# One attention and mixture-of-experts kernel: start-up orders, packing, maxima and the last fetches rescheduled together

## Chip, cores and metric

The kernel runs on one core of a Trainium2 chip. The metric is the device time of one execution in microseconds (us), as the median of three runs. Engines are TensorE (PE), VectorE (DVE), ScalarE (ACT), GpSimd (POOL) and SyncE (SP). SP, ACT and POOL each issue DMAs.

## What is computed

The input is x, 32 sequences of 256 tokens of 128 numbers (8192 tokens). The layer norm of x goes into an attention block and into a block of 8 experts, and both results are added to x:

```python
xn = _layernorm(x, axis=-1)
x = x + attn(xn, Wqkv, Wproj, bproj) + ffn(xn, gate_w, gate_b, w1, b1, w2, b2)
# attn: 16 heads of 8, rotary embedding, key j allowed for query i where j <= i and i - j <= 64
# ffn: top 2 of 8 gates, softmax over the two, out += w_e * (gelu(x @ w1[e] + b1[e]) @ w2[e] + b2[e])
```

## The kernel before, in words

**Units.** The 8192 tokens are NT = 64 tiles of 128. A pair b (0 to 31) is one sequence, two tiles. Attention runs in 128 units u, four to a pair (half of the queries times half of the heads). The maxima of the scores are taken first (`scores`: PE at L575 and L582, DVE reduce at L881). Unit by unit, ten units later, the scores are computed again transposed with the maxima subtracted as extra rows of the product (`scoresT`: PE at L608, L612 and L619), exponentiated on ACT (L1048) and multiplied by the values (`pv`: PE at L635).

**Queries and keys.** For each pair, PE projects (L548), DVE rotates (L854 to L865), PE transposes (L559), and ACT, DVE and POOL split the result in three bfloat16 parts (L1015, L872, L1020, and `lo` on POOL at L1111). SP writes the parts to DRAM with six DMAs (`write`, L419 and L421) and reads them back in another layout with four (`load`, L432). SP also stores the values (`vstore`, L385) and loads them per pair (`vload`, L396 and L398).

**Maxima.** For each pair, DVE splits the maxima in three parts (`msplit`), PE transposes them (`turn_m`, L591), ACT copies them (L1028) and issues their store to DRAM (`mput`, L1032); after a wait for that store ACT issues two DMAs that load them into the rows of QK (`mget`, L1040). `scoresT` of the pair's first unit waits for these loads.

**Norm and routing.** The tiles are normed in groups of up to six (`stats` L720 and L723, `norm` on DVE L729 to L735 and, from the third group on, 14 small operations on POOL, L1090 to L1101; `apply` on POOL L1105 and ACT L976). From quarter 18 on the top two experts of each token are found (`route`) and POOL scatters the normed tiles into expert slots with 128 indirect DMAs (`scatter`, L1168). `pack` copies each expert's weights into one DRAM tensor (L407, L409), together with both biases (L401, L403). The b2 row of each expert is written 128 times there, for one copy per partition.

**Experts.** 71 slots of 256 tokens are computed one after another: SP loads tokens and weights (`eload` L455, `wload` L464), PE transposes (`etr`, L673), multiplies up (L686) and down (L699), ACT applies gelu (L1069), DVE adds and scales (L941, L947) and POOL scatters the rows by token into DRAM (L1174).

**The end.** 32 `fetch` DMAs on SP (L474) bring the two expert rows of each token, POOL adds the two (L1179), DVE adds them to xr (`combine`, L955) and SP stores (L479).

**Order.** `schedule()` writes one list of steps, and every engine goes through it in order, taking its own part of each step. Its clock is the quarter q, from FIRST = -22 to 139. `middle` and `late` give what a quarter does after `scoresT(q)` and `pv(q-1)`, with an offset d: the step is for pair (q+d)//4. `scores(q+10)` stands between them. The experts are placed as one block at q = 105, so the attention of pairs 26 to 31 comes after them. `norm_late` and `put` are functions inside `schedule()`. A semaphore wait stands in front of each step's first instruction, so whatever follows on the same engine waits too. PSUM has eight banks: 0 and 1 hold `scores`, 2 and 3 hold `scoresT`.

Of the kernel before, what the change touches and what calls it, by code (L numbers as in the profile page):

```python
# [17 lines left out]
NG = len(GR) - 1  # L18
NB = len(BT) - 1
# [8 lines left out]
FIRST = -22  # L28
ROUTE = 18
# [3 lines left out]
def schedule():  # L33
# [12 lines left out]
    middle = ((("add", 20), ("out", -4), ("mput", 4), ("residual", -8)), (("hi", 19), ("mget", 3)),  # L46
              (("norm_y", -6), ("rest", 18), ("expand", 2)), (("rope", 21), ("mid", 17)))
# [17 lines left out]
    def norm_late(q):  # L65
# [6 lines left out]

        for g in range(3, NG):
            d = FIRST + 4 * (g - 1) - q
            if 6 <= d <= 8:
                order.append(("stats", g, 8 - d))
            if d == 6:
                order.append(("norm", g))
        for g in range(2, NG):
            d = FIRST + 4 * (g - 1) - q  # L80
            order.extend(("apply", g, j) for j, at in enumerate((4, 3, 2, 2, 1, 0)) if d == at)
# [14 lines left out]
    def put(stages, q):  # L96
        order.extend((what, (q + d) // 4) for what, d in stages[q % 4] if 0 <= (q + d) // 4 < NP)
# [7 lines left out]
    for q in range(FIRST, NU + 12):  # L105
        if q == 4 * CUT + 1:
            order.append(("up", 0))
            for i in range(NS):
                if 4 <= i + 3 < NS:
                    order.extend([("eload", i + 3), ("wload", i + 3)])  # L110
                if i + 2 < NS:
                    order.append(("etr", i + 2))
                if i + 1 < NS:
                    order.append(("up", i + 1))
                order.append(("down", i))
# [12 lines left out]
        put(late, q)  # L128
        norm_late(q)
# [16 lines left out]
        for n in pieces(k - 3):  # L146
# [8 lines left out]
def attention_moe_kernel(nc, x, wqkv, wproj, bproj, gate_w, gate_b, w1, b1, w2, b2, cf, cb, out):  # L155
# [15 lines left out]

    Dst = [nc.dram_tensor(f"stack_{i}", (2, 6, P, 256), bf16).ap() for i in range(3)]
# [5 lines left out]
    Wd = nc.dram_tensor("experts", (NE, P, WE), f32).ap()  # L178

# [3 lines left out]
    with ctx:  # L183
# [112 lines left out]
        d_vl = [semaphore(f"d_vl{i}") for i in range(NV)]  # L296
        d_b, d_bt, e_bt, a_bt, v_wv = (semaphore(n) for n in ("d_b", "d_bt", "e_bias", "a_bias", "v_wv"))
# [43 lines left out]
        yv = Ys[ROW0:, :].rearrange("(t p a) c -> p t a c", p=P, a=2)  # L341
# [8 lines left out]

        def bank(n):
            return (7, 4)[n] if n < 2 else 6 - n % 2

# [17 lines left out]
        def _(e):  # L371
            for g in range(NG):
                e.dma_start(xr[:, GR[g]:GR[g + 1], :], xv[:, GR[g]:GR[g + 1], :]).then_inc(d_x[g], 16)  # L373
            for what, *a in ORDER:
                if what == "ones":
                    e.wait_ge(p_cb, 1)
                    for n in range(NQ):
                        for g in range(2):
                            e.dma_start(QK[64 * g + 48:64 * g + 51, n, 1, :].rearrange("p (r c) -> p r c", c=P),
                                        onesb[0:3, :].unsqueeze(1).broadcast_to((3, 16, P))).then_inc(d_one, 16)  # L380
                elif what == "vstore":
                    n = a[0]
                    u0, m = BT[n], BT[n + 1] - BT[n]
                    e.wait_ge(a_vp, n + 1)
# [14 lines left out]
                elif what == "bias" and a[0] == 2:  # L399
# [3 lines left out]
                    e.dma_start(Wd[:, :, 1028:WE], b2s[:, 0:1, :].broadcast_to((NE, P, P))).then_inc(d_bt, 16)  # L403
                elif what == "pack":
                    ex = a[0]
                    if a[1] == 0:
# [59 lines left out]
                elif what == "fetch":  # L466
# [7 lines left out]
                    e.dma_start(gy[:, k % NF, :, :, :], yv[:, 2 * b:2 * b + 2, :, :]).then_inc(d_g[k % NF], 16)  # L474
# [8 lines left out]
        def _(e):  # L483

            b4, b5, b6, b7 = [], [], [], []
            for what, *a in ORDER:
# [106 lines left out]
                elif what == "scoresT":  # L593
                    b, t, c = a[0] // 4, a[0] // 2 % 2, a[0] % 2
                    s = b % NQ
                    e.wait_ge(d_m[b % 2], 32 * (b // 2 + 1))
                    if a[0]:
# [642 lines left out]
```

## Time and profile before

| what | us |
| --- | --- |
| median of 3 runs | 747.93 (747.35 to 749.89) |
| profiled execution, whole | 751.46 |
| its span, first to last instruction | 749.3 |
| PE, DVE, ACT, POOL busy in the span | 655.8, 479.8, 358.3, 391.8 |
| mean granted PE clock | 0.951 of full |

The span is taken from the trace, and the execution's own time is 2.2 us longer. A busy share is an average over stages that have different limits: the start (to 58 us, where the first `scores` runs), attention beside norm and routing (58 to 209 us), attention beside the scatters (209 to 403 us), the experts (to 673 us) and the last attention units beside the fetches (to 749.3 us).

### The profile page before, as it was taken

To read this page: it belongs to the slowest core of one execution; us is meant where nothing else is said; L and a number is where in the kernel's file an instruction comes from. 1 tells how busy PE (TensorE), PEld (TensorE's weight loads), DVE (VectorE), ACT (ScalarE), POOL (GpSimd) and SP (SyncE) were. 2 spreads that over 40 slices of the span, in tenths; PEclk is the share of its full clock that TensorE was granted. 3 is DMA by queue.
4 is the path that set the end of the run, shared out by engine and by line. 5 is a ranking of instruction groups with operands and counts; after the bars stand their busy time and mean duration, and the time that the engine had idled before them with its cause. 6 is when DMAs were issued, how large, how long until landed. Compare 5 with 4: busy or idle time off the path is not lost.

```text
span 749.3 us, 26576 instructions
## 1 busy us (share of the span) xinstructions
PE 655.8 (88%) x10238; PEld 527.9 (70%) x10238; DVE 479.8 (64%) x1362; ACT 358.3 (48%) x681; POOL 391.8 (52%) x525
## 2 busy tenths in 40 slices
PE   7436799978799898899989799999999999998866
PEld 3324576655566676566657799999999999995654
DVE  6538987699778878777887344444444444446654
ACT  1322576645355555455556344444444444455443
POOL 1563544056777776777660355555555554553344
PEclk8788999999799999999999999999999999999886
DMA  9567899764777877877778777777767676866797
GB/s 259 143 119 209 218 240 258 195 165 133 203 194 211 221 211 191 220 183 203 190 191 246 212 232 232 234 233 236 231 227 234 230 232 208 254 197 159 200 281 240
DMA packets 161436, 158.78 MB, mean 212 GB/s; under 512 B 20328, under 2 KB 140280, under 8 KB 161312
## 3 DMA queue, kind: packets, MB, share of 16 engines
q1 hardware_dynamic: 147504, 136.12, 64.7%
q0 software_dynamic: 8640, 17.97, 7.2%
q10 hardware_dynamic: 5168, 3.00, 1.5%
q8 instruction: 82, 1.34, 0.8%
q14 instruction: 42, 0.34, 0.1%
HBM read 102.06 MB, written 59.06 MB: 215 GB/s over the span
## 4 chain that ended last, share of the span: by engine, by line
PE 54%; DMA 13%; DVE 11%; SPq 8%; issue 7%; ACT 4%; POOL 3%; ACTq 1%; DVEq 0%; POOLq 0%
PE ps L699 17%; PE ps L686 16%; DMA maxima<-mT 9%; DVE mx L881 4%; PE ps L635 4%; POOL slots_x L1168 2%; PE ps L663 2%; SPq L419 2%; SPq L373 2%; PE ps L575 2%; ACT PT L1048 2%; PE ps L619 2%; PE ps L673 2%; PE ps L548 2%; DMA stack<-sp 2%
## 5 line engine op out<-in xcount | busy, mean ns | idle before, releaser
L1174 POOL DMA_INDIRECT chosen_y<-xn,to x142 | 135.9, 957 | 141.3 <-DVE xn L947 117.2
L881 DVE TENSOR_REDUCE mx<-ps 128x8 f32<-128x1024 f32 x128 | 156.4, 1222 | 67.1 <-PE ps L582 65.7
L1048 ACT ACTIVATE PT<-ps 128x1024 f32<-128x1024 f32 x128 | 131.0, 1023 | 135.3 <-PE ps L619 69.2
L1069 ACT ACTIVATE hb<-ps,xn 128x256 f32<-128x256 f32 x284 | 116.6, 470 | 150.9 <-PE ps L686 150.8
L1168 POOL DMA_INDIRECT slots_x<-xn,pos x128 | 125.4, 980 | 55.9 <-issue 33.3
L699 PEld LDWEIGHTS ps<-xn,hb 128*128 128x128 f32 x1136 | 138.7, 193 | 3.7
L699 PE MATMUL ps<-xn,hb 128*128 128x128 f32 x1136 | 138.8, 276 | 0.0
L686 PE MATMUL ps<-xn 128*128 128x256 f32 x568 | 135.4, 381 | 0.0
L686 PEld LDWEIGHTS ps<-xn 128*128 128x128 f32 x568 | 102.9, 191 | 11.2
L941 DVE TENSOR_TENSOR xn<-ps,xn 128x256 f32<-128x256 f32 x71 | 30.1, 424 | 100.3 <-PE ps L699 100.3
L635 PE MATMUL ps<-PT,V 128*32 128x64 f32 (+1 forms) x3072 | 87.8, 247 | 2.7 <-issue 2.7
L575 PE MATMUL ps<-cb_s 64*64 64x512 bf16 x512 | 54.4, 410 | 22.4 <-DMA QK<-stack 12.8
L635 PEld LDWEIGHTS ps<-PT,V 128*32 128x32 f32 x3072 | 58.4, 113 | 12.4 <-issue 2.9
L1111 POOL TENSOR_TENSOR sp<-rr,sp 128x512 bf16<-128x512 f32 x32 | 37.2, 1163 | 48.8 <-ACT sp L1020 48.4
L582 PEld LDWEIGHTS ps<-QK 48*64 48x64 bf16 x2048 | 47.1, 109 | 15.9 <-issue 4.5
L582 PE MATMUL ps<-QK 48*64 48x128 bf16 x2048 | 54.3, 221 | 2.2 <-issue 2.1
L619 PE MATMUL ps<-QK 51*128 51x64 bf16 (+1 forms) x1536 | 53.0, 202 | 1.1 <-issue 1.1
L619 PEld LDWEIGHTS ps<-QK 51*128 51x128 bf16 x1536 | 45.9, 97 | 11.4 <-issue 2.9
L575 PEld LDWEIGHTS ps<-cb_s 64*64 64x64 bf16 x512 | 15.3, 104 | 44.5 <-issue 39.7
L548 PE MATMUL ps<-wq_s,xnT 128*128 128x256 f32 x128 | 40.6, 445 | 6.8 <-ACT Vt L989 6.4
L1179 POOL TENSOR_TENSOR xn<-xn 128x256 f32<-128x256 f32 x32 | 23.9, 760 | 34.1 <-DMA xn<-chosen_y 34.1
L933 DVE TENSOR_TENSOR to<-eq,cf_s 128x2 int32<-128x2 f32 x71 | 11.5, 161 | 40.9 <-DMA chosen_y<-xn,to 39.4
(133 smaller groups left out, 902.2 us busy)
## 6 DMA issues: line engine op xcount, KB each, us to landing
xn<-experts SPq DMA_DIRECT2D x71, 578.0 KB, 3.9
QK<-stack SPq DMA_DIRECT2D x128, 192.0 KB
stack<-sp SPq DMA_DIRECT2D x64, 192.0 KB
xn<-slots_x SPq DMA_DIRECT2D x71, 132.0 KB, 3.4
stack<-sp SPq DMA_DIRECT2D x64, 128.0 KB
xn<-chosen_y SPq DMA_DIRECT2D x32, 256.0 KB, 4.6
stack<-sp SPq DMA_DIRECT2D x64, 64.0 KB
Vc<-values SPq DMA_DIRECT2D x32, 128.0 KB
```

The costliest lines, as they stand in the source:

```text
L548: k = e.matmul(ps[:, 5, t * 256:(t + 1) * 256], xnT[:, c0:c0 + P], wq_s[:, 0:256], start=True, stop=True, skip_group_check=True)
L575: e.matmul(ps[q0:q0 + 64, g, :].rearrange("p (h k) -> p h k", h=4), unit[r:r + 64, 0:64], (win0 if t + blk == 0 else win)[r:r + 64, :].uns ...
L582: k = e.matmul(ps[q0 % P:q0 % P + m, g, h4 * P:(h4 + 1) * P], qk_rows(0, g, 48, s, hh, q0, m), qk_rows(1, g, 48, s, hh, w0, P), start=Fals ...
L619: k = e.matmul(ps[:, 2 + g, h4 * P + q0 % P:h4 * P + q0 % P + m], qk_rows(1, g, 51, s, hh, w0, P), qk_rows(0, g, 51, s, hh, q0, m), start= ...
L635: k = e.matmul(ps[32 * j:32 * j + 32, 4, o0:o0 + n], V[:, b % NV, w, 4 * g + j, 16 * c:16 * c + 32], PT[:, a[0] % 2, i0:i0 + n], start=t + ...
L686: k = e.matmul(ps[:, 2 * s + c // 2, (c % 2) * SL:(c % 2 + 1) * SL], w1b[:, i % NW, c * P:(c + 1) * P], xsT[:, i % 3, :], start=True, stop ...
L699: k = e.matmul(ps[:, bk, j * P:(j + 1) * P], hb[:, s, c, j * P:(j + 1) * P], w2b[:, i % NW, c * P:(c + 1) * P], start=c == 0, stop=c == 3, ...
L881: e.tensor_reduce(mo[:, :, :, c, t], ps[:, 0:2, :].rearrange("p g (h k) -> p g h k", k=P), AX.X, ALU.max, negate=True).then_inc(v_mx, 1)
L1048: e.activation(PT[:, u % 2, :], ps[:, 2:4, :].rearrange("p c k -> p (c k)"), ACT.Exp, scale=SCALE).then_inc(a_exp, 1)
L1069: e.activation(hb[:, s, c, :], ps[:, 2 * s + c // 2, (c % 2) * SL:(c % 2 + 1) * SL], ACT.Gelu, bias=b1b[:, i % NW, c:c + 1]).then_inc(a_ge ...
L1168: e.indirect_dma_start(out=Xs, out_offset=bass.IndirectOffsetOnAxis(ap=pos[:, n, u:u + 1], axis=0), in_=xn[:, u, :], in_offset=None).then_ ...
L1174: e.indirect_dma_start(out=Ys, out_offset=bass.IndirectOffsetOnAxis(ap=to[:, i % 4, j:j + 1], axis=0), in_=yb[:, i % 4, j, :], in_offset=N ...
```

## The change

It consists of these edits, all in one kernel:

- **Norm.** `stats` of groups 4 to 8 are issued two thirds of a group per quarter, from q = -19 to -12; before they were one third per quarter and lasted to q = 0. The `norm` steps work on groups 0, 1, 2, 3, then 4 and 5 together, 6 to 8 together, 9 and 10 (NR). `factors(g)` gives the waits. The `apply` steps of group 2 on ACT are put later.
- **SP's queue at the start.** The eight `ones` DMAs go from SP at q = -19 to ACT, one per quarter from q = -9. The first two `vstore` DMAs are issued by ACT right behind their copies.
- **Packing.** `pack` goes from one DMA per quarter (q = 1 to 16) to one every third quarter. The 512 KB write of b2 from SBUF is replaced by a 4 KB store to DRAM at the start and a broadcast from DRAM to DRAM at q = 49.
- **Maxima.** `mget` goes from q = 4b-3 to q = 4b-2. For pairs 28 to 31 `turn_m`, `mput` and `mget` stand at q = 4b-6, 4b-5 and 4b-3, in place of 4b-5, 4b-4 and 4b-3.
- **Entry to the experts.** `load` and `vload` of q = 103 are held back until slot 2 of the experts, behind `eload` and `wload` of slot 5.
- **Last ten units.** `scoresT` of units 118 to 127 alternates between banks 2, 3 and banks 0, 1 (`stb`), so it waits for the exponential of the unit before the last.
- **Fetches.** The rows of DRAM are laid out so that one partition reads 2 KB in one piece. Two fetches per quarter begin at the seventh fetch instead of the eleventh, and the `combine` steps follow four quarters behind instead of three.

```diff
+NR = (0, 1, 2, 3, 4, 6, 9, 10, 11)
+FREE = 28
-    middle = ((("add", 20), ("out", -4), ("mput", 4), ("residual", -8)), (("hi", 19), ("mget", 3)),
-              (("norm_y", -6), ("rest", 18), ("expand", 2)), (("rope", 21), ("mid", 17)))
+    middle = ((("add", 20), ("out", -4), ("mput", 4), ("residual", -8)), (("hi", 19),),
+              (("norm_y", -6), ("rest", 18), ("mget", 2), ("expand", 2)), (("rope", 21), ("mid", 17)))
...
-        for g in range(3, NG):
-            d = FIRST + 4 * (g - 1) - q
-            if 6 <= d <= 8:
-                order.append(("stats", g, 8 - d))
-            if d == 6:
-                order.append(("norm", g))
+        d = q - FIRST
+        some = [(3, d)] if d < 3 else [divmod(n, 3) for n in (2 * d + 6, 2 * d + 7) if n < 27]
+        some += [(g, 8 - FIRST - 4 * (g - 1) + q) for g in (9, 10) if 6 <= FIRST + 4 * (g - 1) - q <= 8]
+        for g, p in some:
+            order.append(("stats", g, p))
+            if p == 2 and g + 1 in NR:
+                order.append(("norm", NR.index(g + 1) - 1))
...
-        if q == FIRST + 3:
-            order.append(("ones",))
+        if -9 <= q < -9 + 2 * NQ:
+            order.append(("ones", q + 9))
-        if 1 <= q <= 2 * NE:
-            order.append(("pack", (q - 1) // 2, (q - 1) % 2))
+        if q >= 1 and q % 3 == 1 and q // 3 <= 2 * NE:
+            order.append(("pack", q // 3 // 2, q // 3 % 2))
...
+    def maxima(q):
+        for what, d in (("mput", 5), ("turn_m", 6), ("mget", 3)):
+            if (q + d) % 4 == 0 and FREE <= (q + d) // 4 < NP:
+                order.append((what, (q + d) // 4))
     def pieces(k):
-        return [k] if 0 <= k < 10 else [n for n in (2 * k - 10, 2 * k - 9) if n < NP] if k >= 10 else []
+        return [k] if 0 <= k < 6 else [n for n in (2 * k - 6, 2 * k - 5) if n < NP] if k >= 6 else []
...
+                if i == 2:
+                    order.extend(held)
...
+        maxima(q)
+        if q == 4 * CUT - 1:
+            held = [o for o in order if o in (("load", (q + 13) // 4), ("vload", (q + 5) // 4))]
+            order = [o for o in order if o not in held]
...
-        for n in pieces(k - 3):
+        for n in pieces(k - 4):
...
+    TWO = NU - AHEAD
+        def stb(u):
+            return 0 if u >= TWO and (u - TWO) % 2 else 2
...
-                    e.dma_start(Wd[:, :, 1028:WE], b2s[:, 0:1, :].broadcast_to((NE, P, P))).then_inc(d_bt, 16)
+                    e.dma_start(b2d, b2s[:, 0, :]).then_inc(d_b2, 16)
                 elif what == "pack":
                     ex = a[0]
-                    if a[1] == 0:
+                    if ex == NE:
+                        e.wait_ge(d_b2, 16)
+                        e.dma_start(Wd[:, :, 1028:WE], b2d.unsqueeze(1).broadcast_to((NE, P, P))).then_inc(d_bt, 16)
...
-                    e.dma_start(gy[:, k % NF, :, :, :], yv[:, 2 * b:2 * b + 2, :, :]).then_inc(d_g[k % NF], 16)
+                    e.dma_start(xflat[:, k % NF * 512:(k % NF + 1) * 512], yv[b]).then_inc(d_g[k % NF], 16)
...
-                    if a[0]:
+                    if a[0] == TWO + 1:
+                        e.wait_ge(v_mx, NU)
+                    elif a[0] > TWO + 1:
+                        e.wait_ge(a_exp, a[0] - 1)
+                    elif a[0]:
                         e.wait_ge(a_exp, a[0])
...
+                elif what == "ones":
+                    n, g = divmod(a[0], 2)
+                    e.wait_ge(p_cb, 1)
+                    e.dma_start(QK[64 * g + 48:64 * g + 51, n, 1, :].rearrange("p (r c) -> p r c", c=P),
+                                onesb[0:3, :].unsqueeze(1).broadcast_to((3, 16, P))).then_inc(d_one, 16)
...
-                         2.0 * (np.arange(64)[None, :] * 128 + np.arange(128)[:, None]) + ROW0,
+                         2.0 * (np.arange(64)[None, :] // 2 * 256 + np.arange(64)[None, :] % 2 + 2 * np.arange(128)[:, None]) + ROW0,
```

## Rows read from the trace of the kernel before

**Rows 1.** Busy us (x instructions) of each engine by stage, granted clock, DMA share, GB/s

```profile
58.00:86.00 28.00, 19.76 (x300) 14.53 (x300) 26.17 (x76) 10.93 (x25) 13.59 (x37) 0.94 0.79 209
86.00:152.00 66.00, 59.98 (x1302) 44.80 (x1306) 51.07 (x123) 42.71 (x77) 23.49 (x59) 0.97 0.88 230
152.00:209.00 57.00, 45.72 (x1016) 31.71 (x1017) 47.16 (x99) 26.34 (x41) 35.14 (x45) 0.91 0.60 159
209.00:390.00 181.00, 164.19 (x4055) 117.08 (x4049) 146.74 (x256) 102.58 (x159) 130.43 (x131) 0.99 0.76 205
...
419.00:673.00 254.00, 254.00 (x1758) 239.66 (x1757) 116.63 (x536) 111.45 (x272) 127.28 (x133) 0.99 0.72 229
673.00:714.00 41.00, 34.89 (x841) 25.34 (x843) 26.60 (x49) 19.80 (x29) 14.66 (x18) 0.92 0.65 175
714.00:749.30 35.30, 23.74 (x447) 16.70 (x447) 16.56 (x41) 14.23 (x20) 15.13 (x20) 0.73 0.89 265
```

**Rows 2.** Chain that ended last, 20 to 58 us: start us, us, what

```profile
19.42 6.38 DMA values<-Vt
...
37.34 4.75 SPq L419
...
50.01 2.31 DMA stack<-sp
...
53.65 4.30 DMA QK<-stack
```

**Rows 3.** DMA view of 36 to 49 us, in 40 slices

```profile
DMA  0599754444444444444469644444447495445434
GB/s 0 147 235 228 30 21 54 46 50 46 47 46 50 46 47 46 50 46 47 46 120 221 106 46 50 46 47 46 50 46 98 55 195 68 49 54 66 46 41 39
```

**Rows 4.** Timeline of SP, 0 to 130 us: start us, us, engine line operation

```profile
26.80 6.22 SPq L379 DMA_DIRECT2D QK<-cb_s  x8
...
54.58 1.79 SPq L419 DMA_DIRECT2D stack<-sp  x3
56.41 1.55 SPq L421 DMA_DIRECT2D stack<-sp  x3
```

**Rows 5.** Timeline of all engines, 0 to 62 us: POOL's rows

```profile
19.43 0.20 POOL L1090 TENSOR_TENSOR nw<-rs 128x6 f32<-128x6 f32 x1 [6.58 <-DVE rs L735]
...
23.47 0.20 POOL L1101 TENSOR_SCALAR nb<-nb 128x6 f32<-128x6 f32 x1
...
34.20 1.16 POOL L1111 TENSOR_TENSOR sp<-rr,sp 128x512 bf16<-128x512 f32 x1 [3.07 <-ACT sp L1020]
```

**Rows 6.** Groups by line, 58 to 86 us: busy, mean ns | idle before

```profile
L720 DVE BATCH_NORM_STATS2 bst<-xr 128x6 f32<-128x128 f32 x16 | 3.8, 278 | 0.0
```

**Rows 7.** Waits, 209 to 390 us: us in total, times, longest

```profile
ACT PT L1048 <- DMA maxima<-mT: 34.1, 12, 3.5
```

**Rows 8.** What PE at L608 sat idle for, 209 to 390 us

```profile
  ACT PT L1048: 6.5, 10
```

**Rows 9.** Timeline, 208 to 222 us: a load of maxima, and its user

```profile
215.24 0.57 ACTq L1040 DMA_DIRECT2D QK<-maxima  x2
...
219.48 0.11 PEld L612 LDWEIGHTS ps<-cb_s 64*128 64x128 bf16 x4
```

**Rows 10.** Groups by line, 209 to 390 us: the scatters

```profile
L1168 POOL DMA_INDIRECT slots_x<-xn,pos x115 | 112.3, 977 | 51.4 <-issue 30.2 <-PE ps L582 20.0 <-ACT sp L1020 1.2
```

**Rows 11.** Timeline of PE, 409 to 427 us: the stall behind the first slots

```profile
418.63 0.41 PE L673 MATMUL ps<-cf_s,xn 128*128 128x128 f32 x2 [3.81 <-DMA xn<-slots_x]
```

**Rows 12.** Waits, 674 to 749 us

```profile
POOL xn L1179 <- DMA xn<-chosen_y: 34.1, 18, 6.4
...
ACT PT L1048 <- DMA maxima<-mT: 11.1, 3, 4.0
```

**Rows 13.** Timeline, 715 to 750 us: PE behind the last such wait

```profile
728.22 0.61 PE L608 MATMUL ps<-cb_s 64*128 64x512 bf16 x2 [2.88 <-ACT PT L1048]
```

**Rows 14.** Waits of the whole span: DVE on landed expert rows

```profile
DVE to L933 <- DMA chosen_y<-xn,to: 39.4, 43, 3.3
```

More of the change, by code:

```diff
@@ L96, in put @@
     def put(stages, q):
-        order.extend((what, (q + d) // 4) for what, d in stages[q % 4] if 0 <= (q + d) // 4 < NP)
+        for what, d in stages[q % 4]:
+            if 0 <= (q + d) // 4 < (FREE if what in ("turn_m", "mput", "mget") else NP):
+                order.append((what, (q + d) // 4))
+    def maxima(q):
+        for what, d in (("mput", 5), ("turn_m", 6), ("mget", 3)):
+            if (q + d) % 4 == 0 and FREE <= (q + d) // 4 < NP:
+                order.append((what, (q + d) // 4))
     def pieces(k):
-        return [k] if 0 <= k < 10 else [n for n in (2 * k - 10, 2 * k - 9) if n < NP] if k >= 10 else []
+        return [k] if 0 <= k < 6 else [n for n in (2 * k - 6, 2 * k - 5) if n < NP] if k >= 6 else []
     moved, due = 0, 0.0
@@ L178, in attention_moe_kernel @@
     Wd = nc.dram_tensor("experts", (NE, P, WE), f32).ap()
+    b2d = nc.dram_tensor("bias_2", (NE, P), f32).ap()
     Ys = nc.dram_tensor("chosen_y", (ROW0 + 2 * NT * 128, P), f32).ap()
@@ L296, in attention_moe_kernel @@
         d_vl = [semaphore(f"d_vl{i}") for i in range(NV)]
+        d_b2 = semaphore("d_b2")
         d_b, d_bt, e_bt, a_bt, v_wv = (semaphore(n) for n in ("d_b", "d_bt", "e_bias", "a_bias", "v_wv"))
@@ L349, in xn_ready, with factors @@
             return (p_xn, 3 * g + ON_POOL.index(j) + 1) if j in ON_POOL else (a_xn, 3 * g + ON_ACT.index(j) + 1)
+        def factors(g):
+            return max(i for i in range(len(NR)) if NR[i] <= g) - 1
         def bank(n):
             return (7, 4)[n] if n < 2 else 6 - n % 2
+        def stb(u):
+            return 0 if u >= TWO and (u - TWO) % 2 else 2
         def batch(u):
@@ L374, in _ @@
             for what, *a in ORDER:
[L375 to L381, printed above, removed]
+                if what == "vstore":
                     n = a[0]
                     u0, m = BT[n], BT[n + 1] - BT[n]
+                    if n < 2:
+                        continue
                     e.wait_ge(a_vp, n + 1)
@@ L725, in _ @@
                     g = a[0]
[L726 removed]
+                    u0, u1 = GR[NR[g]], GR[NR[g + 1]]
                     y, a_, b_ = nw[:, 0, u0:u1], nw[:, 1, u0:u1], rs[:, u0:u1]
@@ L991, in _ @@
                                  ACT.Copy).then_inc(a_vp, 1)
+                    if n < 2:
+                        e.wait_ge(a_vp, n + 1)
+                        e.dma_start(Vd.rearrange("(t p) c -> p t c", p=P)[:, BT[n]:BT[n + 1], :],
+                                    Vt[:, n % 2, 0:m * P].rearrange("p (t c) -> p t c", c=P)).then_inc(d_vs[n % 2], 16)
                 elif what == "expand":
@@ L1047, in _ @@
                         e.wait_ge(e_pv, u - 1)
-                    e.activation(PT[:, u % 2, :], ps[:, 2:4, :].rearrange("p c k -> p (c k)"), ACT.Exp,
+                    e.activation(PT[:, u % 2, :], ps[:, stb(u):stb(u) + 2, :].rearrange("p c k -> p (c k)"), ACT.Exp,
                                  scale=SCALE).then_inc(a_exp, 1)
```

17 lines of the change are left out of this document (9 added, 8 removed).

## The prediction

> **What bounds the kernel now.** I first cut the span into stages with the view of busy time by window [rows 1]. The experts (419 to 673 us) are PE alone: 254.00 of 254 us busy, at clock 0.99. No edit takes work from that stage, so a third of the time can't move unless DMA gets in its way. Everything to be won lies before and after it. Then I read the chain that ended last in each stage, to see what it hangs on, and the waits and the timeline for the price of each link.
>
> At the start the chain leaves the engines: it is the store of the first values (6.38 us to landing), then SP's issue of the first `write`, whose first DMA alone holds SP for 4.75 us, then its landing and the first `load`, landed at 57.95 us [rows 2]. From 58 to 86 us DVE is the bound, 26.2 of 28 us busy; from 86 to 152 us it is PE (60.0 of 66) with DMA at 0.88; from 152 to 209 us DVE carries the routing (47.2 of 57). From 209 to 390 us PE is busy 164.2 of 181 us, and POOL nearly as much: 130.4 us, plus 30.2 us of issue gaps that stand before its scatters whatever PE does [rows 1, 10]. In the last 76 us PE is busy 58.6 us and the clock falls to 0.73 in the second part [rows 1].
>
> **The change part by part.**
>
> *First write.* Today SP spends 6.22 us on the `ones` DMAs [rows 4] and then sends b2. After that, for some eight microseconds, the DMA view stands at 4 to 5 tenths and 46 to 50 GB/s [rows 3]: half of the 16 DMA engines work, slowly. 512 KB at 47 GB/s are 11.2 us, and the six DMAs of `write` take SP from 37.34 to the last one's issue at 50.01, where an unhindered write needs 1.79 + 1.55 = 3.4 us [rows 2, 4]. That b2 is the cause I infer from its size. The edit takes away all three: `ones`, b2, and (with the stores of the values on ACT) the place of the values behind the x loads. I take the values' landing 3.4 us earlier, half of the 6.38 us that it took [rows 2], between nothing and all of it. But POOL gets a new step in front: `norm` of groups 4 and 5 now stands before the first `lo`, and such a norm takes 4.2 us (19.43 to 23.67) on POOL [rows 5]. So `lo`, now at 34.20, would be at 34.2 - 3.4 + 4.2 = 35.0 if DVE had the statistics ready; DVE must do six more pairs of tiles before it, and I put `lo`'s end at 38.7 us. Then 3.4 us of issue, 2.3 - 0.5 to landing, 1.7 of issue of the loads and 4.3 - 0.4 to landing give about 49.8 us against 57.95. **-8 us** (bounds -3, if only b2's obstruction is half gone, and -13, if `lo` keeps to 35.0).
>
> *Statistics out of DVE's tight stage.* From 58 to 86 us 16 tiles' statistics fall, 3.8 us at L720, with aggregation at some two thirds of that again, about 6.3 us in all (an estimate), and the small norm operations [rows 6]. They move to before 58 us, where SP and DMA hold the chain [rows 2]. DVE being the bound, this would give 6; PE and the turn-taking of PE and DVE over banks 0 and 1 take the rest. **-4** (-1 to -7).
>
> *Packing thinned, 86 to 152 us.* DMA falls from 0.88; PE, 60.0 of 66 us busy, leaves 6 at most [rows 1]. **-3** (0 to -6). In the routing stage nothing moves but `mget`: **-1** (0 to -4).
>
> *Maxima, 209 to 390 us.* ACT waits 34.1 us in 12 places because `mget` stands in its queue while the store of the maxima is still on its way, and the exponential is behind it [rows 7]. That looks like the prize, but PE works on meanwhile: it pays 6.5 us in 10 places [rows 8]. With `mget` one quarter later the exponential goes first. POOL would then be next: 115 scatters and the `lo`s fill 181 - 20.0 = 161 us, so the stage can't shrink by more than 20, and 16.8 us is PE's own idle time [rows 1, 10]. **-6** (0 to -15).
>
> *b2 again, q = 49.* The broadcast has the same 8 x 128 x 512 bytes, now in the midst of attention. The `load` behind it, two quarters later, has three quarters (8 us) until it is used and needs about 4.3 [rows 2]; a queue of 11.2 us would be half over. **+1** (0 to +8).
>
> *Here a rule speaks against the change.* The row shows half of the DMA share while b2 is out [rows 3]. The Trainium skill, "DMA: Bandwidth & Descriptors", section "Why a DMA increments its semaphore by 16 and not by 1", says that a DMA from SP or ACT is spread over the largest number of DMA engines, up to 16, that divides the slowest dimension on both sides; by that rule, the trace agrees, and the broadcast from DRAM, whose slowest dimension is still 8, keeps 8 engines. The sum would have +8 there by the rule at its hardest, and +1 by my reading.
>
> *Entry to the experts.* PE stands 3.81 us before slot 4's tokens, because SP is held by `load` and `vload`, behind `write` [rows 11]. Holding these loads frees SP. **-4** (-2 if the slot's own tokens still come late, -6 if the clock, which falls where PE pauses as in the last stage [rows 1], comes back sooner too).
>
> *The end.* For pairs 28 to 31 the store of the maxima leaves one quarter earlier, so ACT's waits (11.1 us, 3 times [rows 12]) go; here PE is not full and pays nearly all, 2.88 us at the last [rows 13]: 8.5 us. Two banks for the last ten units and the higher clock of a busier PE give some 4 more, since now each exponential and each `scoresT` take turns. Against that stands DMA, 0.89 busy at 265 GB/s in the last 35 us [rows 1]: this fixes how fast fetches and stores go by, and POOL already waits 34.1 us for fetches [rows 12]. Pieces of 2 KB help. **-9** (-3 to -14).
>
> *At nothing:* `apply` of group 2 moved (ACT waits there anyway), `ones` on ACT (eight issues in quarters in which ACT is busy 10.9 of 28 us [rows 1]); without that cover, 6 us.
>
> **Sum:** -8 - 4 - 3 - 1 - 6 + 1 - 4 - 9 = -34. The profiled execution's own time is 751.5, giving 717.5; it stands 3.5 us above the median of the runs, so the median becomes 747.9 - 34 = **714**.
>
> **The rivals.**
>
> 1. *Maxima come late.* They are now asked for closer to their use. Today 3.7 us lie between the end of the issue (215.81) and the first use (219.48) with no wait shown [rows 9], so landing takes less, but PE would be 0.7 us sooner. If landing takes 3.5 us, PE waits about as long as it gained, and the 7 us of stages 152 to 390 are not won: 721; with stores that take longer, 724.
> 2. *b2 obstructs in its new place* as in the old one, +8 instead of +1: 721.
> 3. *The end is bound by DMA.* The attention units run ahead and then wait for fetches; -3 instead of -9: 720. For: the share of 0.89. Against: only 0.65 before 714 us, and fetches that start denser there [rows 1].
> 4. *More is won:* PE's idle time of 209 to 390 us goes nearly whole and the end gives 14: 714 - 9 - 5 = 700.
> 5. *Slower.* The new layout puts the rows that L1174 scatters further apart. DVE already waits 39.4 us for their landing [rows 14], and DVE has to be done with a slot in 3.7 us (1758 PE instructions at 26 per slot are 68 slots in 254 us), of which it is busy 1.7 [rows 1]. If landing grew by over 2 us, PE would start to wait, 71 times; at another 0.6 us per slot that is +43, and 757. Nothing shows it: the rows stay 512 bytes.
>
> **Chances.** Forecast 0.55 (own range 705 to 724); rivals 1 and 2 0.12 and 0.10; rival 3 0.10; rival 4 0.08; rival 5 0.03; several of 1 to 3 at once and more give-backs, ending near 730 or at no change, 0.02. The range runs from 700 to 731. A measurement of this kernel tells about 0.3% (2.2 us) from no change. Faster 0.95, same 0.02, slower 0.03.
>
> **What would show it.** First `scores` at about 50 us; its `write` in 3.4 us of SP. DVE under 0.85 busy in the ten quarters after. ACT's wait for the store of maxima nearly gone from 209 us on, PE over 0.94 busy and the scatters without a wait for PE. No stall of 3.8 us behind the first slots. From the last slot to the end about 67 us instead of 76, clock above 0.85. Wrong would be: a wait of L612 for QK<-maxima in most pairs (rival 1), a `scores` that waits for QK<-stack near q = 53 (rival 2), an unchanged 76 us at the end with POOL waiting for fetches (rival 3), slots of over 3.8 us (rival 5).

## The result and the profile after

The changed kernel takes **728.49 us** (median of four runs, 721.15 to 731.24), the kernel before 747.64 (four runs, 746.68 to 749.89): a ratio of 0.9719, interval 0.9666 to 0.9772. Forecast were 714 in a range of 700 to 731. The sign and the range held, the size did not: about 19 to 20 us were won where 34 were said. The four runs of the changed kernel lie 10 us apart, those of the kernel before 3.

The clearest ruler for a kernel in which one engine does 128 like steps is the time at which given steps start. The exponentials on ACT (one per attention unit) are such steps. The profile of before, timeline of ACT, the exponentials of units 0, 20, 36, 100 and 127 (the experts come between 104 and 108); a line ends with ACT's idle time before it and what ended it:

```profile
85.74 1.02 ACT L1048 ACTIVATE PT<-ps 128x1024 f32<-128x1024 f32 x1
...
152.01 1.02 ACT L1048 ACTIVATE PT<-ps 128x1024 f32<-128x1024 f32 x1 [1.79 <-PE ps L619]
...
209.39 1.02 ACT L1048 ACTIVATE PT<-ps 128x1024 f32<-128x1024 f32 x1 [1.72 <-PE ps L619]
...
392.00 1.03 ACT L1048 ACTIVATE PT<-ps 128x1024 f32<-128x1024 f32 x1 [0.85 <-PE ps L619]
...
739.31 1.02 ACT L1048 ACTIVATE PT<-ps 128x1024 f32<-128x1024 f32 x1 [0.51 <-PE ps L619]
```

And of after (the line is L1095 there; the same units):

```profile
75.47 1.02 ACT L1095 ACTIVATE PT<-ps 128x1024 f32<-128x1024 f32 x1
...
137.00 1.02 ACT L1095 ACTIVATE PT<-ps 128x1024 f32<-128x1024 f32 x1 [1.79 <-PE ps L656]
...
194.27 1.02 ACT L1095 ACTIVATE PT<-ps 128x1024 f32<-128x1024 f32 x1 [1.54 <-PE ps L656]
...
379.40 1.03 ACT L1095 ACTIVATE PT<-ps 128x1024 f32<-128x1024 f32 x1 [0.90 <-PE ps L656]
...
716.97 1.02 ACT L1095 ACTIVATE PT<-ps 128x1024 f32<-128x1024 f32 x1 [0.18 <-PE ps L656]
```

Their differences, with the first `scores` (58.08 us before, 50.05 after) and the ends of the spans (749.3 and 729.0), give a table that adds up to the whole:

| stretch | before | after | difference | forecast |
|---|---|---|---|---|
| start to the first `scores` | 58.1 | 50.1 | -8.0 | -8 |
| to exponential 0 | 27.7 | 25.4 | -2.2 | -4 |
| exponentials 0 to 20 | 66.3 | 61.5 | -4.7 | -3 |
| 20 to 36 | 57.4 | 57.3 | -0.1 | -1 |
| 36 to 100 | 182.6 | 185.1 | +2.5 | -6 + 1 |
| 100 to 104 | 10.3 | 10.2 | -0.2 | |
| 104 to 108, the experts between | 282.0 | 279.1 | -2.8 | -4 |
| 108 to 127 | 55.0 | 48.3 | -6.7 | -9, with the next |
| 127 to the end | 10.0 | 12.0 | +2.0 | |
| sum | 749.3 | 729.0 | -20.3 | -34 |

(Differences are taken before rounding. The profiled execution of after took 731.24 us, the slowest of its four; that of before, 751.46, was the slowest too.) So 7.5 of the 13.7 missing us are lost between exponentials 36 and 100, and 4.3 after 108.

The engines by stage in after answer to [rows 1]; columns as there:

```profile
50.00:75.30 25.30, 20.35 (x279) 14.98 (x279) 20.70 (x37) 10.62 (x24) 9.33 (x11) 0.88 0.78 208
75.00:137.00 62.00, 59.14 (x1334) 44.44 (x1332) 50.65 (x118) 43.19 (x78) 21.27 (x46) 1.00 0.86 215
137.00:194.00 57.00, 45.43 (x1018) 31.72 (x1021) 47.24 (x99) 26.53 (x41) 35.37 (x45) 0.91 0.68 186
194.00:379.00 185.00, 166.10 (x4084) 119.25 (x4078) 147.65 (x257) 106.13 (x160) 130.24 (x132) 0.97 0.80 212
391.00:660.00 269.00, 265.38 (x1849) 250.32 (x1847) 123.74 (x566) 119.32 (x288) 132.38 (x139) 1.00 0.73 229
660.00:729.00 69.00, 49.88 (x1261) 35.11 (x1259) 44.25 (x86) 32.54 (x47) 28.32 (x37) 0.92 0.80 238
```

In the second row PE is busy 59.1 of 62 us: that stage is now PE's. In the fourth it still stands 18.9 us, in the last 19.1.

The chain of after, 20 to 60 us, beside [rows 2]: from POOL's last norm operation and `lo` to the first `scores`, with no gap for b2.

```profile
38.21 1.13 POOL sp L1158
39.36 0.38 SPq L451
...
41.52 0.69 SPq L453
42.25 1.72 DMA stack<-sp
...
44.82 1.44 SPq L464
46.30 3.62 DMA QK<-stack
50.05 0.64 PE ps L607 x4
```

`write` now needs 2.9 us from first issue to landing's start (12.7 us before). **Waits** of 194 to 379 us, beside [rows 7] and [rows 8]:

```profile
POOL slots_x L1215 <- issue: 30.1, 91, 4.9
PEld ps L607 <- issue: 24.0, 37, 3.9
ACT V L1042 <- DMA Vc<-values: 19.6, 11, 3.6
...
PE ps L607 <- issue: 12.7, 8, 3.7
...
ACT V L1042 <- DMA maxima<-mT: 3.6, 3, 1.6
PE ps L607 <- DMA QK<-stack: 2.9, 2, 1.5
```

ACT's wait for the store of the maxima, 34.1 us in 12 places before the exponential, is down to 3.6 in 3, all before another instruction. In its place ACT waits 19.6 us for `values`, and PE stands in front of L607, the first matmul of `scores`, 15.6 us in 10 places (12.7 + 2.9), most of its idle time; before the change it stood 2.8 us in front of that matmul (L575) from exponential 36 to 100. SP's own waits between exponentials 36 and 100 say what the `load` came behind. In the kernel before, L428 is its wait for a free QK buffer and L432 that for the landed `write`:

```profile
SPq L428 <- PE ps L619: 27.7, 14, 4.7
...
SPq L432 <- DMA stack<-sp: 8.8, 9, 1.7
```

and in after (L460 and L464):

```profile
SPq L464 <- DMA stack<-sp: 25.6, 14, 2.9
SPq L460 <- PE ps L656: 23.1, 13, 4.3
```

### The profile page after: what moved, and what is told of

Read it like the earlier page. It is cut to its first block, busy times and chain, and to the rows that moved or that the text cites. A ratio compares the mean times of both kernels' runs of the same rounds, so it can differ in the third digit from the quotient of the medians.

```text
span 729.0 us, 26522 instructions
## 1 busy us (share of the span) xinstructions
PE 648.6 (89%) x10234; PEld 523.8 (72%) x10238; DVE 479.2 (66%) x1353; ACT 360.9 (50%) x681; POOL 385.0 (53%) x483
## 4 chain that ended last, share of the span: by engine, by line
PE 67%; DVE 15%; DMA 6%; issue 6%; SPq 3%; POOL 2%; ACTq 0%; ACT 0%; DVEq 0%; POOLq 0%
PE ps L736 17%; PE ps L723 16%; PE ps L672 7%; DVE mx L918 6%; PE ps L607 5%; PE ps L614 3%; PE ps L580 3%; PE ps L656 3%; PE ps L700 2%; PE ps L649 2%; PE ps L710 2%; PE ps L591 2%; DMA QK<-stack 2%; PE ps L645 1%; DMA stack<-sp 1%
## 5 line engine op out<-in xcount | busy, mean ns | idle before, releaser
L1095 ACT ACTIVATE PT<-ps 128x1024 f32<-128x1024 f32 x128 | 131.0, 1023 | 89.6 <-PE ps L656 82.9
L672 PE MATMUL ps<-PT,V 128*32 128x64 f32 (+1 forms) x3072 | 85.3, 244 | 4.6 <-ACT PT L1095 1.8
L607 PE MATMUL ps<-cb_s 64*64 64x512 bf16 x512 | 54.3, 413 | 26.9 <-issue 15.1
L672 PEld LDWEIGHTS ps<-PT,V 128*32 128x32 f32 x3072 | 57.1, 111 | 15.4 <-ACT PT L1095 3.4
L1158 POOL TENSOR_TENSOR sp<-rr,sp 128x512 bf16<-128x512 f32 x32 | 37.7, 1178 | 55.8 <-ACT sp L1062 55.3
L656 PEld LDWEIGHTS ps<-QK 51*128 51x128 bf16 x1536 | 45.0, 96 | 10.2 <-issue 1.3
L607 PEld LDWEIGHTS ps<-cb_s 64*64 64x64 bf16 x512 | 15.5, 104 | 47.2 <-issue 43.0
L970 DVE TENSOR_TENSOR to<-eq,cf_s 128x2 int32<-128x2 f32 x71 | 11.5, 161 | 43.3 <-DMA chosen_y<-xn,to 41.4
L1226 POOL TENSOR_TENSOR xn<-xn 128x256 f32<-128x256 f32 x32 | 23.6, 756 | 29.8 <-DMA xn<-chosen_y 29.6
```

Of the source, the lines that this page charges most:

```text
L607: e.matmul(ps[q0:q0 + 64, g, :].rearrange("p (h k) -> p h k", h=4), unit[r:r + 64, 0:64], (win0 if t + blk == 0 else win)[r:r + 64, :].uns ...
L656: k = e.matmul(ps[:, B + g, h4 * P + q0 % P:h4 * P + q0 % P + m], qk_rows(1, g, 51, s, hh, w0, P), qk_rows(0, g, 51, s, hh, q0, m), start= ...
L672: k = e.matmul(ps[32 * j:32 * j + 32, 4, o0:o0 + n], V[:, b % NV, w, 4 * g + j, 16 * c:16 * c + 32], PT[:, a[0] % 2, i0:i0 + n], start=t + ...
L1095: e.activation(PT[:, u % 2, :], ps[:, stb(u):stb(u) + 2, :].rearrange("p c k -> p (c k)"), ACT.Exp, scale=SCALE).then_inc(a_exp, 1)
```

## The experiments

These ran on chips on which the kernel before took longer than the 747.6 us above: 796.5 us for the first four runs (13 runs of before), 793.6 for the next four, 758.1 for the last four. Ratios are to those; stage times are best compared within such a group. The first group and the last ran on a chip that bears the same number, so "a slower chip" stands below for a slower group of runs: whether it was another chip or another hour isn't shown. Only the first group has a run of the changed kernel as it is, and none has a profile of the kernel before. The profile of the changed kernel in the first group differs in one stage above all: exponentials 36 to 100 take 222.9 us instead of 185.1.

**The changed kernel again.**

> The changed kernel unaltered, as the reference for the runs beside it. Its four runs so far spread from 721.2 to 731.2 us, so I expect a median of 721 to 731. Quarter 36 to quarter 100 took 185.1 us in its profile (before: 182.6); if that is the kernel's own rhythm and no accident of one execution, it is again 180 us or more. First scores at 50 us, and a loss of 3 us or more between quarters 44 and 56, behind the broadcast of b2.

776.90 us, ratio 0.9729 (0.9649 to 0.9808): the same gain, on a chip 6.5% slower, so the 721 to 731 us expected missed. Exponentials 44 to 56 took 42.9 us. First `scores` 48.8 us, exponential 0 at 73.9, span 775.0. In its waits, 185 to 408 us, PE and ACT stand in other places than above:

```profile
POOL slots_x L1215 <- PE ps L614: 64.9, 46, 2.7
ACT PT L1095 <- remote: 25.9, 11, 2.7
...
PEld ps L607 <- issue: 20.4, 60, 1.1
```

The longest wait before L607 is 1.1 us, against 3.9: here many small stalls bind, not a few long ones. What a run of this group says of stage 36 to 100 doesn't carry over to the faster chip without a doubt.

**Maxima: back to three quarters' lead, and moved alone.**

```diff
-              (("hi", 19),), (("norm_y", -6), ("rest", 18), ("mget", 2), ...
+              (("hi", 19), ("mget", 3)), (("norm_y", -6), ("rest", 18), ...
```

> The changed kernel with the loads of the maxima (pairs below 28) asked for three quarters ahead again. Theory A (from quarter 36 on the bound is now the round trip of queries and keys through DRAM: lo, write, load, scores; the exponential was free anyway): ACT's wait for the store of the maxima is back at 30 us or more, and the time stays within 3 us of the changed kernel. Theory B (my prediction's: the exponential held up behind mget costs PE 0.6 us a pair): 6 us or more slower. Theory C (maxima asked for late make scoresT wait): 3 us or more faster.

778.65 us, 0.9723 (0.9663 to 0.9783): no difference from the changed kernel. ACT's wait for the store was only 7.5 us in this run (30 or more were expected), since units come more slowly on this chip (3.5 us each in that stage, 2.9 on the faster), so this doesn't price the edit where the wait is 34 us.

The other way round, `("mget", 2)` in place of `("mget", 3)` as the one edit to the kernel before:

> The kernel before with one edit: the loads of the maxima asked for two quarters ahead. Theory A: ACT's wait of 51.7 us for the store of the maxima nearly goes, and the whole becomes at most 3 us faster (745 or more). Theory B: 6 to 12 us faster (736 to 742). Theory C: slower, with a wait of L612 for the loads of the maxima.

794.77 us, 0.997 (0.9928 to 1.0012; ten runs). Moved alone it brings nothing that can be measured on this chip; there the 2.7% are won by the rest. PE waits 3.9 us in two places at L612 for `QK<-maxima`, the sign of rival 1; in the profile of after it doesn't.

This run is also the nearest thing to a profile of the kernel before in this group (its profiled execution, 787.8 us, is 7 us faster than its median). Beside the changed kernel (`after_again`) its stages read:

| stretch | `mget_alone` | `after_again` |
|---|---|---|
| start to exponential 0 | 85.0 | 73.9 |
| exponentials 0 to 20 | 61.8 | 61.6 |
| 36 to 100 | 223.4 | 222.9 |
| 104 to 108, the experts between | 280.4 | 286.4 |
| 108 to the end | 62.5 | 59.1 |

So what the start wins here (11.0 us) is as much as the two profiles differ in all (10.6). Between exponentials 0 and 20 the packing and the statistics stand where they stood before, and still the stretch is only 0.2 us longer. And the experts take 6.0 us more in the changed kernel: with the loads in their old place, PE never waited for a slot's tokens here; with them held, it waits 2.7 us.

**b2: sent in the start after all.** The broadcast to the eight experts stands again where it did, the changed kernel otherwise as it is.

```diff
+ e.dma_start(Wd[:, :, 1028:WE], b2s[:, 0:1, :].broadcast_to((NE, P, P))).then_inc(d_bt, 16)
  e.dma_start(b2d, b2s[:, 0, :]).then_inc(d_b2, 16)
...
- e.dma_start(Wd[:, :, 1028:WE], b2d.unsqueeze(1).broadcast_to((NE, P, P))).then_inc(d_bt, 16)
+ pass
```

> The changed kernel with the 512 KB write of b2 from SBUF back at the start, and nothing at quarter 49. If that write alone held up the first write of the stack: first scores at 57 to 60 us instead of 50. If the broadcast at quarter 49 costs what the profile shows (some 4.6 us between quarters 44 and 56), these come back, and the whole is 3 to 5 us slower than the changed kernel; if the loss there has another cause, 8 to 10 us slower. If the removal of the ones DMAs from SP was what mattered at the start, no change there and 4 us faster in all.

783.06 us, 0.980 (0.9737 to 0.9864). The timeline of SP:

```profile
33.59 4.92 SPq L433 DMA_DIRECT2D bias<-b2s  x1
38.56 7.74 SPq L452 DMA_DIRECT2D stack<-sp  x3
46.34 1.78 SPq L454 DMA_DIRECT2D stack<-sp  x3
```

`write` takes SP 9.6 us, behind 4.9 for the small store of b2 that stands between (in the kernel before, with nothing between, `write` took 13.1), and the first `scores` come at 55.3 instead of 48.8 us: **6.5 us** for this one DMA. Exponential 0 comes 6.6 us later and the span ends 4.8 us later. That b2 was the cause, inferred from its size only, is shown.

**b2 over 16 engines.** In its new place (q = 49) the broadcast with partitions as the outer dimension instead of experts.

```diff
- e.dma_start(Wd[:, :, 1028:WE], b2d.unsqueeze(1).broadcast_to((NE, P, P))).then_inc(d_bt, 16)
+ e.dma_start(Wd[:, :, 1028:WE].rearrange("e p c -> p e c"),
+             b2d.unsqueeze(0).broadcast_to((P, NE, P))).then_inc(d_bt, 16)
```

> The changed kernel with the broadcast of b2 at quarter 49 written with the 128 copies as the slowest dimension instead of the 8 experts. If the loss between quarters 44 and 56 comes from that DMA filling the queues of 8 of the 16 DMA engines: the DMA view shows no stretch at half share there, and the time from quarter 44 to quarter 56 drops by 2 us or more; whole 0.965 to 0.970 of the kernel before (changed kernel: 0.972). If the loss is only jitter of the round trip of queries and keys: no change beyond 1 us in the mean.

778.41 us, 0.9774 (0.9697 to 0.9852): the whole doesn't tell them apart. Between exponentials 44 and 56, where the broadcast falls, it took 40.6 us, against 41.8 to 44.0 in the three other kernels of its group, which all have the broadcast over 8 experts. In the first group it was 42.9 and 42.8 with that broadcast, and 41.6 and 42.1 in the two kernels that send b2 in the start. So about 1 us hangs on the broadcast in the first group, and 1 to 3 on its form in the second, each from single profiles.

**Packing every quarter again.** `pack` in quarters 1 to 16 instead of every third.

```diff
-        if q >= 1 and q % 3 == 1 and q // 3 <= 2 * NE:
-            order.append(("pack", q // 3 // 2, q // 3 % 2))
+        if 1 <= q <= 2 * NE:
+            order.append(("pack", (q - 1) // 2, (q - 1) % 2))
+        if q == 49:
+            order.append(("pack", NE, 0))
```

> The changed kernel with the 16 packing DMAs in quarters 1 to 16 again, one each, and b2 at quarter 49 as it is. My prediction's step: quarter 0 to quarter 20 takes 3 us more than the changed kernel's 61.5 us. Rival: the DMAs only moved their load into the stage that lives on the round trip through DRAM, so that quarters 20 to 48 become 2 to 4 us shorter and the whole stays at 0.972.

780.54 us, 0.9789 (0.9706 to 0.9871). Exponentials 0 to 20 took 62.8 us instead of the 61.6 of two others in this group: thinning is worth about 1.2 us here, less than the 3 forecast. `mget_alone`, with the old packing, took 61.8, so it may be less still. Exponentials 20 to 48 took 103.1 us against 101.9 to 103.6 in the others: the rival's 2 to 4 us less aren't there.

**`lo` and `write` one quarter earlier.** The round from `lo` through DRAM to the `load` gets a quarter more.

```diff
-    late = ((("turn_qk", 20), ("lo", 16)), (("turn_o", -5), ("msplit", 7), ("write", 15)),
-            (("qk", 22), ...), (("load", 13), ..., ("turn_m", 5)))
+    late = ((("turn_qk", 20), ("write", 16)), (("turn_o", -5), ("msplit", 7)),
+            (("qk", 22), ...), (("load", 13), ..., ("turn_m", 5), ("lo", 17)))
```

> The changed kernel with lo right behind mid, ahead of that quarter's scatters, and its write one quarter earlier. Theory A (the round trip lo, write, load, scores bounds quarters 36 to 100, and it begins late because lo stands behind scatters on POOL): SP's wait of 37.9 us for the landed write in front of the loads falls by half or more, quarters 36 to 100 take 175 us or less instead of 185, whole 0.960 of before or less. Rival D (the loads wait for the QK buffer, that is for scoresT three quarters before their use, whatever the write does): same 185 us.

785.59 us, 0.9868 (0.979 to 0.9945): slower than the two runs above (its fastest, 784.9 us, against their slowest, 783.5). The first `scores` come at 45.03 us, 3.0 earlier than in `b2_on_16`, and exponential 0 at 68.57, 4.9 earlier, but 36 to 100 (189.65 to 424.76) takes 235.1 us instead of the 220.4 to 223.3 of the others in its group. SP's wait for the landed `write`, only 9.4 us in all in `after_again`, is 5.7 here, and its wait for a free QK buffer goes from 84.6 to 151.8. So on this chip it is rival D's wait that stands in front of the loads, and theory A's forecast of a faster stage missed.

The start still has 3 to 5 us to give; why the middle pays 12 or more for it isn't settled (POOL, which runs both `lo` and the scatters, gets them in another order).

**`scores` nine quarters ahead instead of ten.** `load` gets a quarter more to land before its use.

```diff
-AHEAD = 10
+AHEAD = 9
...
-  (("turn_o", -5), ("msplit", 7), ("write", 15)), (("qk", 22), ("turn_y", -6))
+  (("turn_o", -5), ("write", 15)), (("qk", 22), ("msplit", 6), ("turn_y", -6))
```

> The changed kernel with scores nine quarters ahead of scoresT instead of ten (msplit one quarter later). This gives each load one more quarter until its first scores, and takes one from the maxima. Theory A and rival D both: PE's waits in front of L607 (36.7 us from quarter 36 to 100) nearly go, and the stage takes 175 us or less. If POOL's scatters are the bound (they wait for scores, which come one quarter later), the stage stays at 185 us. If the maxima become the bound, ACT waits for their store again by 30 us or more.

785.10 us, 0.9869 (0.9772 to 0.9967). 36 to 100 took 222.3 us, as in the others, and the wait for issue before L607 in that stretch stayed: 26.2 us (21.2 of weight loads, 5.0 of matmuls) against 29.2 in `after_again`. One quarter more in front of the `load` brings nothing on such a chip, whose stalls there are the short ones.

**No held load.** `load` and `vload` go out in their place, in front of the expert slots' tokens.

```diff
         if q == 4 * CUT - 1:
-            held = [o for o in order if o in (("load", ...), ("vload", ...))]
-            order = [o for o in order if o not in held]
+            held = []
```

> The changed kernel without holding back load and vload at the entry to the experts. My prediction's step: the stretch from the first transpose of a slot to the last down product (268.9 us in the changed kernel's profile, 271.6 before) becomes 4 us longer, with a wait of slot 4 for its tokens. Rival: the held loads only move the stall to slot 6 (2.8 us there), so without them the stretch changes by 1 to 3 us, either way, and where SP happens to be early it gets shorter, to the 266 us without any stall.

738.51 us, 0.9763 (0.9704 to 0.9822; before 758.05). PE's timeline behind the first slots, beside [rows 11]:

```profile
410.37 0.66 PE L712 MATMUL ps<-cf_s,xn 128*128 128x128 f32 x2 [5.24 <-DMA xn<-slots_x]
```

The stall is back, 5.24 us, and from the first expert transpose to the last `down` 273.4 us pass, against 269.4 and 271.3 in the next two runs and 268.9 in the profile of after: the holding is worth 2 to 4 us in this group. In the first group a kernel without it (`mget_alone`) had no such stall at all, and its block took 4.4 us less than that of `after_again`, so the gain isn't shown for that chip.

**One bank for the last ten units.**

```diff
-    return 0 if u >= TWO and (u - TWO) % 2 else 2
+    return 2
```

(with the matching waits: every unit waits for the exponential before it).

> The changed kernel with all scoresT in banks 2 and 3. My prediction's step: units 116 to 127 take 3 to 4 us more than the 25.2 to 25.5 us of the changed kernel, and the whole 3 us more. Rival (the end hangs on the fetches): the units take longer, but from the last exponential to the end it is then less than the 12.0 us of the changed kernel, so that the whole changes by under 2 us.

731.12 us, 0.9689 (0.961 to 0.9767). Units 116 to 127 take 26.5 us, 1 us more where 3 to 4 were forecast (27.8 in `no_hold`, which has the two banks), and from exponential 108 to the end 57.8 us pass (`no_hold`: 59.9, after: 60.3). The two banks bring nothing that can be seen. This was one of the two things that the forecast's term for the end rested on.

**Fetches sooner.** The pairs of fetches begin after two single ones instead of six, and `combine` waits one quarter longer.

```diff
-        return [k] if 0 <= k < 6 else [n for n in (2 * k - 6, 2 * k - 5) if n < NP] if k >= 6 else []
+        return [k] if 0 <= k < 2 else [n for n in (2 * k - 2, 2 * k - 1) if n < NP] if k >= 2 else []
...
-        for n in pieces(k - 4):
+        for n in pieces(k - 5):
```

> The changed kernel with two fetches per quarter from the third on and the combines five quarters behind. If the end hangs on the fetches because SP stands at stores that wait for late combines while the next fetches queue behind them: POOL's wait for fetches falls from 29.6 us below 20, from the last exponential to the end it takes 10 us instead of 12, and the whole is 2 to 4 us faster. If DMA bandwidth is the bound (0.88 busy): no change.

731.82 us, 0.9679 (0.9625 to 0.9733), which isn't told apart from `one_bank`. From 108 to the end 57.1 us, of which 9.6 behind the last exponential, where 10 were expected; but with the fetches as they were it is 10.1 (`no_hold`) and 10.5 (`one_bank`) in this group. POOL still waits for its fetches, in the waits of the whole span:

```profile
POOL xn L1226 <- DMA xn<-chosen_y: 24.9, 16, 5.1
```

29.6 us in the changed kernel, 29.0 in `no_hold` and 27.6 in `one_bank`; under 20 was expected, so this missed. That the fetches are late because they are asked for late explains a few us at most.

**The held load in four parts, with the fetches sooner.** One of its four DMAs behind each of slots 2 to 5, `vload` at slot 6.

```diff
-                if i == 2:
-                    order.extend(held)
+                if 2 <= i <= 5:
+                    order.append(held[0] + (i - 2,))
+                if i == 6:
+                    order.append(held[1])
```

> As fetch_ahead, and the held load is issued in four pieces, one per slot from slot 2, with vload at slot 6. If the stall at slot 6 comes from 768 KB asked for at once ahead of a slot's tokens: no wait of L710 for tokens, 266 to 267 us from first transpose to last down product, and 2.5 us less than fetch_ahead alone.

728.49 us, 0.9629 (0.9538 to 0.972), the lowest median of its group (that it equals the median of after is chance); its interval overlaps those of `one_bank` and `fetch_ahead`, so the whole doesn't tell them apart. Expert block 266.3 us; no PE instruction behind the first slots waits for tokens, where `no_hold` waits 5.24 us, `fetch_ahead` 3.2 and after 2.8. From 108 to the end 57.6 us pass, as in the two runs before it, so what it gains lies in the expert block, 5.0 us less than in `fetch_ahead`. Stage 36 to 100 (188.9 us) is no better.

## Why the prediction was right and where it failed

**Right: the start.** The sum (3.4 us of issue, landing, 1.7 of issue, landing) gave 49.8 us for the landing of the loads, and the trace has 49.92; `lo` ended at 39.3 for 38.7 forecast. POOL's norm operations ahead of `lo` waited for DVE's statistics until 33.76 us, as the sum had it, and took 4.5 us (33.76 to 38.21) for the 4.2 taken from [rows 5]. The landing of the values no longer stands in this chain. The statistics out of DVE's stage gave 2.2 us for 4. That b2 held up the first `write` is confirmed by its experiment (6.5 us there). The Trainium skill, "DMA: Bandwidth & Descriptors", section "Why a DMA increments its semaphore by 16 and not by 1", says that such a DMA runs on the largest number of engines, up to 16, that divides the slowest dimension on both sides; [rows 3] agree (half of the share). Neither showed what mattered most, that the first three DMAs issued behind it in the same queue hold SP for 7.74 us.

**Near in number, by another cause: packing, -3.** Exponentials 0 to 20 gave 4.7 us, but the rows don't give them to the packing. `pack_early` prices it at 1.2 us, `mget_alone` at 0.2 together with the statistics. The kernel before, 86 to 152 us, has the wait for the maxima here too, in front of a copy (L989) for which PE waits:

```profile
ACT Vt L989 <- DMA maxima<-mT: 7.0, 2, 3.5
...
PE ps L548 <- ACT Vt L989: 3.2, 3, 1.5
```

and after, 75 to 137 us:

```profile
PE ps L580 <- ACT Vt L1026: 0.2, 1, 0.2
```

These 3.0 us and PE's busy time, 60.0 to 58.7 us at a granted clock of 0.97 and then 1.00, make 4.3 of the 4.7. So the move of `mget`, for which the forecast put nothing in this stage, is the likelier cause, and that the number came near was luck. It is a reading of rows: no run on the faster chip moved `mget` alone.

**Right: the side things.** The row layout of `chosen_y` brought no slowdown: DVE waits 41.4 us for landings (39.4, [rows 14]), a slot still takes 3.7 us. It brought no quicker fetch either: from issue to landing the median is 4.7 us with pieces of 2 KB and 4.6 without, where the forecast counted on some help. ACT's wait for the maxima went from 58.7 us in the whole span to 6.9.

**Failed step 1, "Maxima, 209 to 390 us: -6".** The forecast gave PE back the 6.5 us that it paid behind ACT's wait [rows 8], and took as next bound POOL's scatters, from which it saw up to 20 us of room. What the runs showed: PE's idle time in that stage went from 16.8 to 18.9 us, so that it is busy 0.90 of it where over 0.94 was forecast. The 6.5 us behind ACT's wait went, and the stalls in front of `scores` grew from 2.8 to 15.6 us. In the timeline of PE in after:

```profile
247.22 0.62 PE L607 MATMUL ps<-cb_s 64*64 64x512 bf16 x4 [3.67 <-issue]
```

and what SP did just before (the broadcast of b2 is L437):

```profile
236.21 0.83 SPq L437 DMA_DIRECT2D experts<-bias  x1
240.05 1.76 SPq L464 DMA_DIRECT2D QK<-stack  x4
```

The `load` at L464 was issued at 241.8 and its `scores` started at 247.2, 5.4 us later. In the chain that ended last, 194 to 379 us, the whole round stands twice; once as

```profile
266.32 1.19 POOL sp L1158
...
270.83 3.56 DMA stack<-sp
...
275.94 5.21 DMA QK<-stack
281.24 0.41 PE ps L607 x4
```

A `load` stands in SP behind the landing of its `write`, and that behind `lo`; between exponentials 36 and 100 SP's wait for that landing grew from 8.8 to 25.6 us. But it stands as long for the other condition of the `load`, a free QK buffer (23.1 us; 27.7 before), which comes from `scoresT` and not from the round. By this reading the round lo, store, load, scores had little slack left before, too (in the chain of before, 209 to 390 us, it stands once, beside waits for the maxima that make 22% of it), and the maxima's wait hid that; I had named POOL as next, not this round through DRAM. This reading is the wait rows' in five executions of kernels of the changed kind on faster chips (181.2 to 188.9 us, always with 7 to 13 us of waits for issue at the matmul of L607 and 15 to 20 for `values`). A spread of 7.7 us among them means that the +2.5 itself is not clear of noise; but none comes to the 177.6 us that the forecast makes. It was **not** confirmed by an experiment: the two runs that gave the round more time ran where other stalls bind, and neither gained; one of them showed SP waiting for the QK buffer instead. Open, too, is the price of `mget` alone on a fast chip, since only one profile of before exists there.

**Rival 2, b2 in its new place.** The stall of 3.67 us comes right behind the broadcast, and exponentials 44 to 56 take 38.8 us (34.1 before; 36.7 to 40.5 in the four kernels of the last group, which all have the broadcast there). The runs on the slower chips put it at 1 to 3 us; so the +1 forecast was too small by at most 4, and the rival's +8 wrong. That leaves part of the 4.6 us unexplained.

**Failed step 2, "The end: -9", was -4.7** (-6.7 up to exponential 127, +2.0 behind it). Two of its parts held: ACT's wait for the maxima went from 11.1 us to 3.3, in one place, and the clock is 0.92 for the 69 us (0.92 and 0.73 in the two parts before). Two did not: the two banks bring nothing (`one_bank`), and fetches remain a bound, as rival 3 said. The chain that ended last, 690 to 729 us:

```profile
707.27 0.41 SPq L511
...
708.36 4.70 DMA xn<-chosen_y
713.13 0.73 POOL xn L1226
...
715.16 1.09 SPq L511
...
716.82 4.08 DMA xn<-chosen_y
```

Here each fetch stands behind a store (L511) in SP's queue. SP's own timeline shows where it stands:

```profile
688.49 1.86 SPq L506 DMA_DIRECT2D xn<-chosen_y  x4
694.19 1.77 SPq L511 DMA_DIRECT2D out<-xr  x3
696.02 1.84 SPq L506 DMA_DIRECT2D xn<-chosen_y  x2
```

From 690.4 to 694.2 us SP waits with a store for its `combine`, and the fetches of the next pieces are queued behind it. I had read the order of stores and fetches but not that a store's wait holds the fetch. Asking for them sooner (`fetch_ahead`) gave an end of 57.1 us for 60.3, but `one_bank` and `no_hold`, with the fetches as they were, have 57.8 and 59.9, so this can't be told from nothing. That the order of stores and fetches costs time is read from these rows; no run changed it alone.

**Failed step 3, "Entry to the experts: -4", was -2.8.** Of this, 1.0 us is the stall (3.81 and 2.77 us) and 1.7 us PE's busy time in the block (267.2 and 265.5 us). The stall didn't go; it moved from slot 4 to slot 6, behind the held load itself, whose four DMAs take SP 1.77 us. Splitting it (`split_and_fetch_ahead`) removes it whole, and the block takes 266.3 us. The step named the cause but not that the held load is itself a queue in front of the tokens.

## What to carry to other kernels

A wait in one engine's list is worth only what the bounding engine pays behind it, and before that is booked as gain, the next chain that passes through DRAM has to be timed against the new, faster rhythm: here, as the wait rows read, the round from `lo` to `scores` took up what the maxima's wait gave back. A term that comes out near its number still needs its cause looked up: the stretch of the packing gained more than forecast, and hardly by the packing. Look at what each shared DMA queue issues ahead of the transfer that is needed: one DMA of 512 KB in 512-byte pieces held six shorter ones behind it and the first `scores` came 6.5 us later, a load moved behind the first tokens stalled the tokens two slots later until it was cut in four, and a store that waits for a result keeps back the fetches behind it.

## What the runs showed of the hardware that was not expected

The kernel before took 747.6, 758.1, 793.6 and 796.5 us in its four groups of runs, each within 2% in itself, and the ratio of the changed kernel was 0.972 and 0.973 in the first and the last. The ratio of the whole carried over where the time didn't, but that of the stages did not: on the slowest, the start alone won 11.0 us and the experts lost 6.0, if `mget_alone` stands for the kernel before. The difference in time sits mostly in the stage where POOL scatters rows by index: 185.1 us for exponentials 36 to 100 on the first, 222.9 on the last, with the granted clock nearly the same (0.97 and 0.96) and DMA moving less (windows of the changed kernel, 195 to 418 us, on the slower chip):

```profile
195.00:418.00 223.00, 192.12 (x4080) 130.55 (x4072) 145.00 (x256) 106.51 (x160) 132.49 (x131) 0.96 0.69 175
```

PE is busy 26 us longer for the same matmuls (4080 against 4084 instructions), and ACT has waits of up to 2.7 us whose releaser is outside the profile ("remote"). What causes them wasn't found. And one DMA that reads b2 and writes 1024 pieces of 512 bytes (8 experts x 128 partitions) holds up SP's issue of the ones behind it, 4.92 us for the first store behind the broadcast and then 7.74 us for the first three DMAs of `write`, where such three DMAs else take 1.8.
